# Mask bias made on GpSimd from spread bytes instead of a TensorE product, in a cross-attention and mixture-of-experts kernel

## What is computed

```python
scores = einsum('bsd,bmd->bsm', layernorm(x), ctx) / sqrt(512)
scores = where(mask[:, None, :], scores, -1e30)        # mask: 64 x 128 booleans
out = softmax(scores) @ ctx, zeroed for a batch whose mask is all false
x = x + out
x = x + ffn(layernorm(x))    # 8 experts, the 2 best of each row, with LoRA parts
```

## Time and profile before

| what | value |
|---|---|
| median of 3 runs | 519.83 us (519.33 to 519.91) |
| profiled execution, span from first to last instruction | 517.7 us (its own time is not given apart) |
| TensorE busy | 497.9 us |
| VectorE busy | 468.4 us |
| ScalarE busy | 352.5 us |
| GpSimd busy | 286.4 us |
| moved by DMA | 189.12 MB |

### The profile page before, as it was taken

One profiled execution on the slowest core, in us unless ns is written; L12 is line 12 of the kernel. 1 busy time (PEld: TensorE's weight loads), 2 busy tenths in 40 slices (PEclk: granted clock), 3 DMA queues, 4 the chain that ended last, 5 costly groups with the idle time before them and its releaser, 6 DMA issues.

```text
span 517.7 us, 16681 instructions
## 1 busy us (share of the span) xinstructions
PE 497.9 (96%) x4040; PEld 434.7 (84%) x4040; DVE 468.4 (90%) x1921; ACT 352.5 (68%) x991; POOL 286.4 (55%) x398
## 2 busy tenths in 40 slices
PE   7999999999999999899999999999999999999994
PEld 6788888888888787688888899999998999999992
DVE  5899999999999997879998999998998999999995
ACT  4778888888888788777777787787444444444441
POOL 4227666777777667765544444444444445454454
PEclk9999999999999999999999999999999999999998
DMA  8999999999999998999999999968999999999942
GB/s 308 332 366 336 382 384 390 388 387 382 392 380 406 381 338 246 332 377 392 410 413 412 411 409 387 366 263 283 410 414 416 418 414 417 416 415 415 380 172 74
DMA packets 65610, 189.12 MB, mean 365 GB/s; under 512 B 9582, under 2 KB 9710, under 8 KB 65520
## 3 DMA queue, kind: packets, MB, share of 16 engines
q1 hardware_dynamic: 44352, 120.20, 62.2%
q0 software_dynamic: 20800, 67.65, 32.7%
q10 hardware_dynamic: 368, 0.22, 0.1%
HBM read 114.04 MB, written 78.73 MB: 372 GB/s over the span
## 4 chain that ended last, share of the span: by engine, by line
PE 68%; DVE 8%; issue 8%; ACT 6%; DMA 5%; SPq 3%; POOL 0%; POOLq 0%; ACTq 0%; DVEq 0%
PE rd L520 9%; PE bank L520 9%; PE bank L366 8%; PE bank L498 8%; PE rd L411 5%; PE rd L536 5%; PE rd L537 4%; PE bank L345 4%; DMA z_own<-z_rows 4%; PE rd L412 4%; PE bank L379 3%; ACT xn L614 2%; PE rd L527 2%; DVE z_shared L1117 2%; SPq L302 2%
## 5 line engine op out<-in xcount | busy, mean ns | idle before, releaser
L684 ACT COPY hT<-bank 128x512 f32<-128x512 f32 x140 | 81.9, 585 | 52.9 <-PE bank L498 52.0
L366 PE MATMUL bank<-cc_sb,xnT 128*128 128x136 f32 x512 | 80.9, 286 | 0.0
L520 PE MATMUL bank<-wg_sb,hT 128*128 x560 | 80.3, 287 | 0.4 <-ACT hT L684 0.4
L520 PE MATMUL rd<-wg_sb,hT 128*128 x560 | 80.2, 286 | 0.0
L1222 POOL DMA_INDIRECT x_rows<-xe x64 | 65.2, 1018 | 26.5 <-issue 20.4
L520 PEld LDWEIGHTS bank<-wg_sb,hT 128*128 128x128 f32 x560 | 72.6, 190 | 0.6 <-issue 0.6
L520 PEld LDWEIGHTS rd<-wg_sb,hT 128*128 128x128 f32 x560 | 72.6, 190 | 0.1
L366 PEld LDWEIGHTS bank<-cc_sb,xnT 128*128 128x128 f32 x512 | 68.5, 191 | 1.9
L536 PE MATMUL rd<-dn_a,ggT_a 128*128 x140 | 67.0, 479 | 2.7 <-DVE ggT_b L1107 1.9
L1237 POOL DMA_INDIRECT out_x<-z_shared x41 | 39.9, 974 | 43.9 <-DVE z_shared L1117 39.8
L1117 DVE SCALAR_TENSOR_TENSOR z_shared<-rd,z_shared 128x512 f32<-128x512 f32 x77 | 57.6, 748 | 1.9 <-PE rd L537 0.2
(11 more groups left out here) (169 smaller groups left out, 1192.0 us busy)
## 6 DMA issues: line engine op xcount, KB each, us to landing
cc_sb<-in_cc SPq DMA_DIRECT2D x64, 532.0 KB, 6.2
z_shared<-z_rows SPq DMA_DIRECT2D x41, 516.0 KB, 19.2
x_sb<-in_x SPq DMA_DIRECT2D x64, 256.0 KB, 5.7
z_own<-z_rows SPq DMA_DIRECT2D x29, 516.0 KB, 19.8
z_shared<-x_rows SPq DMA_DIRECT2D x36, 260.0 KB, 12.3
z_own<-x_rows SPq DMA_DIRECT2D x34, 260.0 KB, 12.5
z_rows<-pad SPq DMA_DIRECT2D x8, 516.0 KB, 8.2
wg_sb<-in_wg SPq DMA_DIRECT2D x8, 288.0 KB, 5.8
```

The costliest lines, as they stand in the source:

```text
L366: mm = pe.matmul(sc_ps[:, 0:S + E], xnT[:, n % 2, k, :], by_feature(n, k, S + E), start=False, stop=(k == KD - 1))
L520: mm = pe.matmul(gu_ps[q % 2][:, 0:GU], hT[:, q % 2, k, :], wg_flat[:, bass.ds(at + k * GU, GU)], start=(k == 0), stop=(k == KD - 1))
L684: act.copy(hT[:, q % 2, :, :], hT_ps[q % 2][:].rearrange("p (k s) -> p k s", k=KD)).then_inc(hT_ready, 1)
```

## The change

The mask product on TensorE and `tile_of` go. SyncE loads the mask's bytes eight times 8 batches with a broadcast over the partitions, so that every partition holds the whole mask; the bytes lie in the idle halves of `z_own`. The bias of four batches, (mask - 1) x 1e30 in bf16 on all 128 partitions, is made by one instruction over 512 elements: for batches 0 to 3 on VectorE, for the others on GpSimd, into a ring of 4 in `hT`. VectorE's `mask_scores` adds it in place of the zeros. ScalarE waits, ahead of the experts' stage, until the bias and its readers are done.

```diff
+RX, RC, RE, RB = 11, 6, 16, 4
+MB = 8
-            bias, valid = sb_of(sweep, "bias", [S + E], BF16), sb_of(sweep, "valid", [B])
+            valid = sb_of(sweep, "valid", [B])
+        def mask_of(n, count):
+            slot, at = divmod(n * S, 4 * D)
+            return z_own[:, slot, 0:D].bitcast(U8)[:, at:at + count * S]
+        bias = hT[:].rearrange("p a k s -> p (a k s)").bitcast(BF16)
+        def bias_of(n, count):
+            return bias[:, n % (RB * TB) * S:(n % (RB * TB) + count) * S]
 # SyncE
+            def spread_mask(i):
+                rows = mask[i * MB:(i + 1) * MB, :].rearrange("(o b) s -> o (b s)", o=1)
+                sp.dma_start(mask_of(i * MB, MB), rows.broadcast_to([P, MB * S])).then_inc(mask_spread[i], 16)
             load_x(2)
+            spread_mask(0)
             load_cc(0)
...
                     load_x(n + 6)
+                if n % 6 == 0 and n // 6 in range(1, B // MB):
+                    spread_mask(n // 6)
 # TensorE, scores(n)
-                else:
-                    pe.wait_ge(bias_ready, 2)
-                    pe.wait_ge(before_ready, 1)
-                pe.matmul(sc_ps[:, 0:S + E], tile_of[:, n:n + 1].broadcast_to([P, S]), bias[:], start=True, stop=False)
...
-                    mm = pe.matmul(sc_ps[:, 0:S + E], xnT[:, n % 2, k, :], by_feature(n, k, S + E), start=False, stop=(k == KD - 1))
+                    mm = pe.matmul(sc_ps[:, 0:S + E], xnT[:, n % 2, k, :], by_feature(n, k, S + E), start=(k == 0), stop=(k == KD - 1))
 # ScalarE
-            act.copy(tile_of[:], ident[:, 0:B]).then_inc(before_ready, 1)
...
+            act.wait_ge(bias_ready, NB - 1)
+            act.wait_ge(masked_ready, B)
             normalise(0)
 # VectorE, mask_rows()
-                dve.memset(bias[:], 0.0).then_inc(bias_ready, 1)
-                dve.wait_ge(any_ready, 1)
-                dve.wait_ge(bias_ready, 1)
-                dve.tensor_scalar(bias[0:B, 0:S], mask_sb[0:B, :], any_sb[0:B, :], BIG, ALU.subtract, ALU.mult).then_inc(bias_ready, 1)
+                dve.wait_ge(mask_spread[0], 16)
+                dve.tensor_scalar(bias_of(0, TB), mask_of(0, TB), 1.0, BIG, ALU.subtract, ALU.mult).then_inc(bias_first, 1)
 # VectorE, mask_scores(n)
+                if n < TB:
+                    dve.wait_ge(bias_first, 1)
+                else:
+                    dve.wait_ge(bias_ready, n // TB)
-                dve.tensor_tensor_reduce(masked[:, n % 2, :], sc_ps[:, 0:S], zeros[:], -SCALE, 3e38, ALU.add, ALU.min,
+                dve.tensor_tensor_reduce(masked[:, n % 2, :], sc_ps[:, 0:S], bias_of(n, 1), -SCALE, 3e38, ALU.add, ALU.min,
 # GpSimd
+            def mask_bias(m):
+                pool.wait_ge(mask_spread[m * TB // MB], 16)
+                if m >= RB:
+                    pool.wait_ge(masked_ready, TB * (m - RB + 1))
+                pool.tensor_scalar(bias_of(m * TB, TB), mask_of(m * TB, TB), 1.0, BIG, ALU.subtract, ALU.mult).then_inc(bias_ready, 1)
...
+            mask_bias(1)
             for t in range(SWEEP):
                 if t % TB == 2 and t // TB + 1 in range(2, NB):
                     x_scale(t // TB + 1)
+                if t % TB == 0 and t // TB + 1 in range(2, NB):
+                    mask_bias(t // TB + 1)
```

More of the change, by code:

```diff
@@ L81 @@
 RANKED, SHARED, PACE, TABLE, SKIP = 1, 5, 3, 27, 34
-RX, RC, RE = 11, 6, 16
+RX, RC, RE, RB = 11, 6, 16, 4
+MB = 8
 assert RC % 2 == 0
@@ L128, in xattn_moe @@
         ident = const_sb[:, IDENT:IDENT + P]
-        before, after, ones, tile_of = sb("before", [P], BF16), sb("after", [P], BF16), sb("ones", [P], BF16), sb("tile_of", [B], BF16)
+        before, after, ones = sb("before", [P], BF16), sb("after", [P], BF16), sb("ones", [P], BF16)
         base = sb("base", [2 * E], BF16)
         nhalf = sb("nhalf", [2, TB])
-        pad, zeros = sb("pad", [ZW]), sb("zeros", [S])
+        pad = sb("pad", [ZW])
         t1 = sb("t1", [2, KG])
@@ L189, in xattn_moe @@
         mask_loaded = sem("mask_loaded")
+        mask_spread = [sem(f"mask_spread{i}") for i in range(B // MB)]
         set_up, ones_set, pad_set, before_ready = sem("set_up"), sem("ones_set"), sem("pad_set"), sem("before_ready")
@@ L193, in xattn_moe @@
         xT_done, xnT_ready, scores_done = map(sem, ("xT_done", "xnT_ready", "scores_done"))
-        any_ready, valid_done, valid_ready, bias_ready = map(sem, ("any_ready", "valid_done", "valid_ready", "bias_ready"))
+        any_ready, valid_done, valid_ready, bias_first, bias_ready = map(sem, ("any_ready", "valid_done", "valid_ready", "bias_first", "bias_ready"))
         masked_ready, prob_ready, rinv_ready = map(sem, ("masked_ready", "prob_ready", "rinv_ready"))
@@ L429, in rank @@
                 if m == 0:
-                    pe.wait_ge(before_ready, 3)
+                    pe.wait_ge(before_ready, 2)
                     pe.matmul(counted, ones[:], base[:].rearrange("p (b f) -> p b f", b=1).broadcast_to([P, TB, 2 * E]), start=True, stop=False, skip_group_check=True)
@@ L994, in keep_table @@
                                 rt_ps[KEPT:KEPT + 1, at:at + 2 * (hi - lo)].rearrange("p (k q) -> p k q", k=2)).then_inc(tabT_ready, 1)
-            dve.memset(zeros[:], 0.0)
             dve.memset(g_strip[:, :, E:GP], 0.0).then_inc(g_centred, 1)
```

## The result

The changed kernel takes **527.12 us** (median of 4 runs, 526.27 to 528.61); the kernel before took 519.65 beside it. The ratio is 1.0139, with a 95% interval of 1.0115 to 1.0164. The forecast was 518.5 with a range to 520.4: wrong in sign and outside its range. The profiled execution is the longest of the four (528.61 us); its span is 526.3, against 517.7, so the traces show 8.6 us more where the medians show 7.5.

What follows compares the result with a forecast made beforehand. It took TensorE as busiest, VectorE little less, nothing far from its limit. Mask product -1.8, first spread load +0.4, TensorE and ScalarE +0.1, the rest 0, gave -1.3 us: from 519.8 to 518.5, range 516.4 to 520.4.

Steps and rivals of the forecast that it cites:

- The mask product, -1.8: TensorE in the sweep: two of every four removed 0.056 us products lie on the path, 1.8 us less, bounds 0 and 3.6.
- GpSimd's bias, cost 0: GpSimd in the sweep, 15 times: 0.6 us each, between 0.298 and 1.27, fits its idle time, so no one waits.
- The cover: GpSimd's idle time waiting for VectorE at L1180, taken as 34.8 us over 14, 2.5 each, to hide the bias.
- The second spread load, cost 0: Mask bytes for batches 8 to 11: landing near 27.1 us, in time for GpSimd's bias; landing 1.5 later costs that once.
- The first spread load, +0.4, at most 0.93: SyncE's queue at the start, between x(2) and cc(0): 128 KB delays the ring fill by 0.4 us, at most 0.93.
- my sign that a later fill reaches the path: Start: VectorE's wait before the statistics for x(10) at 19.64 was read as showing that a later ring fill costs time.
- VectorE's mask add: VectorE in the sweep: adds bias instead of zeros at the same length; cost 0, and 0.05 more each still fits.
- ScalarE's waits: ScalarE ahead of the first block's normalise: two added waits, long met; TensorE and ScalarE changes together 0 to 0.1, taken 0.1.
- TensorE's weight loads: TensorE in the sweep: the scores' first long load, 191 ns against 96 for the mask's, may lie open; not priced.
- The rule against the change: TensorE after waits for L593: without the product the long weight load lies open; nothing to 0.056 each, at most 0.9 worse.
- Rival 3, 0.13: GpSimd's bias stops VectorE in the sweep: slower, 522 us at 0.9 us per bias, 528 at 1.27; chance 0.13.
- what would show it: Trace signs expected: 64 fewer TensorE instructions, period 12.7 instead of 12.8 us, statistics 0.4 later, GpSimd's bias under 1.3 us.

Runs made afterwards that it cites:

- b_pool_half: Kernel before plus 15 unused GpSimd subtract-and-multiply instructions on 256 of the 512 elements, at the bias's places; ratio 1.0121 to the kernel before.
- a_copy: Changed kernel with GpSimd's biases as plain copies, so batches 4 to 63 go unmasked; ratio 1.0177 to the kernel before.
- b_load_warm: Kernel before plus only the first spread load, read by nobody, and 40 small matmuls in TensorE's gap at the start; ratio 1.0021.
- a_dve_order: Changed kernel with all 15 biases on VectorE, the first behind the statistics of x(3), and the first spread load behind x(3); ratio 1.0082 to the kernel before.
- b_load_spare: Kernel before plus only the first spread load, between x(2) and cc(0), into an idle place nobody reads; ratio 1.0099.
- a_same: Changed kernel, unaltered, run again on another chip; ratio 1.0145 to the kernel before on that chip.
- a_order: Changed kernel with the first spread load behind x(3) and VectorE's first bias behind the statistics of x(3); ratio 1.0122 to the kernel before.

## Why the prediction was wrong, by its steps

- *(The mask product, -1.8.)* On the first chip the pace of batches 8 to 26 agrees (0.127 per period, forecast 0.112), and it brings 0.57 us. Then GpSimd sets the pace, and the rest is never seen. On the other chips, with nothing else changed, the readouts show 0.1 us for the 64 products (chip 2) and 0.35 (half of two, chip 7): the term was too large there.
- *(GpSimd's bias, cost 0.)* **This step failed first.** "I take 0.6", with 1.27 as the upper end: it took 1.94, and "cost 0" became 3.0 us over batches 26 to 63. The ends came from rows of other operations, and two inputs of 512 floats were no upper bound for one input with two operations. The cover was misread too. "34.8 over 14, or 2.5 each" is a mean over two waits of 7.75 and 7.23 us at the start and 1.3 to 2.0 in the rest, 1.61 in most periods. By its length 1.27 would still have fitted, and 1.94 doesn't fit in 1.61. That fitting is enough isn't shown: on another chip 1.07 us left GpSimd a wait in every other period and cost 6.5 us all the same (b_pool_half).
- *(The second spread load, cost 0.)* The chain was right and it had the answer in it: "if it lands 1.5 us later, that much once". It was issued at 26.41, not 21.8, since the start had moved, landed after 7 us instead of 5.3, and the bias behind it was 1.3 us longer than the 0.6 I took. The price was 2.2 us, by a_copy mostly the bias.
- *(The first spread load, +0.4, at most 0.93.)* **The largest miss**: 4.6 us. I priced 128 packets by their bytes or by a mean packet. Alone it costs 1.8 us of landing time (b_load_warm against the runs with no load at the start), and the gap that it opens lets the clock fall for 2.0 more. That is 3.8 of the 4.6, from another chip; what the rest is isn't shown. It need not be VectorE's first bias, 0.43 us: on the other chips the load alone has batch 0 at 20.95 and the whole change at 20.82. What I costed at nothing was the queue behind the load: cc(0), for which TensorE waits, lands 1.85 us later. The clock was in no term at all, though rows 9 show TensorE only 3.76 of 5 us busy at that place. And my sign that a later fill reaches the path, VectorE's 0.34 us before the statistics at 19.64, has VectorE's own L728 as what ended it, not a load.
- *(VectorE's mask add, ScalarE's waits, TensorE's weight loads.)* The mask add takes 0.282 us on average in both traces. The rule against the change came out at its lower bound, nothing: where TensorE waits for L593, the first long product starts 0.14 instead of 0.20 us after that wait's end, so the longer weight load takes nothing back.
- *(Rival 3, 0.13.)* Right side, wrong mechanism. Its own price at 1.94 us would be 15 x 1.29 - 1.3, or 18 us more; the spans differ by 8.6, most of it from other places. VectorE keeps its lengths beside the bias. GpSimd stopped the sweep by its own queue, not through VectorE. The Trainium skill (Advanced Engine Details and Errata, GPSIMD Details) names as conflicting VectorE's instructions with two inputs in SBUF or in a two-port mode. That the statistics (0.68) and the readout (0.75, one input in PSUM) keep their length agrees with it. The 1.52 us bias of a_dve_order is a case of the two engines stopping each other that the kernel after doesn't have. Of "what would show it", the period (13.2, not 12.7) and the bias's length (1.94, not under 1.3) were the rows that gave the verdict.

## What to carry to other kernels

Take an engine's spare time from the steady period's own row in the timeline, never from a sum over the waits: two long waits at the start made 1.6 us look like 2.5. Then treat a fit as necessary and not as enough: an instruction that fits can still move others. An operation that has no row of its own form has no upper bound from rows of other forms, and the chance of a loss must say so. A load put ahead of the first operand of the first matmuls is priced by what it delays and by the clock behind the gap, and a matmul of 56 ns hidden in a stream is a small prize beside that.

## What the runs showed that I had not expected

- A two-operation instruction of GpSimd on 128x512 takes 1.92 to 1.95 us whatever the types, 0.65 on 128 and 1.07 on 256; with one operation 1.49; a plain copy 0.61.
- Spreading 1 KB over 128 partitions delays the load behind it by some 1.8 us at the start of this kernel. While it runs the rate is 270 GB/s (the kernel after) or 285 (b_load_warm), where it was 360.
- A stand of TensorE of 2.5 to 2.9 us at 8 us goes with 10.2 us at 1.2 GHz (the kernel after) or 6.8 (b_load_spare, a_same). Forty matmuls in the gap keep 2.4 GHz. A gap of 0.73 us went with the loss in a_order and without it in a_dve_order.
- VectorE's two-operation instruction on 128x512 took 1.52 us instead of 0.39 when it started 0.03 us behind GpSimd's sum of two 128x512 inputs, in two traces of two.
- On the chips where this kernel takes 3.5% longer, about one in ten of TensorE's recorded completion signals in the sweep comes 0.2 to 2.3 us after its matmul's end, more often when that end falls into one of GpSimd's scatters; on the first chip none does. The shorter of two added instructions on GpSimd cost more there than the longer one (6.5 and 2.8 us on one chip); that the place of the scatters does it is a guess.
